# Rows 2 and 3 of a fused attention kernel: one tile of each pair transposed by VectorE and DMAs, diagonal blocks handled over their used columns, new timetables

## The reference

```
xn = layernorm(x)                                  # 8 x 1024 x 256
q = (xn @ Wq + bq) in 8 heads of 128, + positions  # one shared key/value head
k, v = xn @ Wkv + bkv, k + positions
scores = q k^T / sqrt(128), causal; probs = softmax(scores)
attn = (probs @ v) of 8 heads, side by side, @ Wo
r = sigmoid(xr @ W_r^T); kk = relu(xk @ W_k^T)^2   # xr, xk mix a token with the one before
out = x + attn + r * (kk @ W_v^T)
```

## Time and profile before

| | us |
|---|---|
| median of 3 runs (1560.83 to 1561.88) | 1561.39 |
| the profiled execution's own time | 1561.37 |
| its span in the profile | 1559.6 |
| PE busy | 1533.5 (98%) |
| PE weight loads busy (PEld) | 1497.6 (96%) |
| DVE busy | 1210.4 (78%) |
| ACT busy | 1056.2 (68%) |
| POOL busy | 1060.7 (68%) |

### The profile page before, as it was taken

How to read it: one execution, slowest core, us unless ns; L and a number is a source line. 1 busy time by engine, 2 the same in 40 slices (tenths; PEclk the granted TensorE clock), 3 DMA queues, 4 the chain that set the end, 5 groups by cost and what they waited for, 6 DMA issues and landing times.

```text
span 1559.6 us, 35317 instructions
## 1 busy us (share of the span) xinstructions
PE 1533.5 (98%) x12032; PEld 1497.6 (96%) x12032; DVE 1210.4 (78%) x3284; ACT 1056.2 (68%) x2531; POOL 1060.7 (68%) x1549
## 2 busy tenths in 40 slices
PE   5999999999999999999999999999999999999998
PEld 5999999999999999999999999999999999999998
DVE  6888767887678876788768787688876888768875
ACT  5776667766667766677577676676766677666764
POOL 5666776667756777567775676756766577765765
PEclk8999999999999999999999999999999999999999
DMA  4014420244202441024410244103431034300443
GB/s 139 9 53 121 146 75 22 58 122 148 69 15 69 129 143 55 15 75 134 144 42 15 86 141 127 42 15 98 140 129 32 12 112 138 129 20 8 119 147 105
DMA packets 151425, 132.46 MB, mean 85 GB/s; under 512 B 12240, under 2 KB 146512, under 8 KB 151248
## 3 DMA queue, kind: packets, MB, share of 16 engines
q1 hardware_dynamic: 150672, 129.55, 27.0%
q10 hardware_dynamic: 576, 0.66, 0.1%
HBM read 67.25 MB, written 62.91 MB: 83 GB/s over the span
## 4 chain that ended last, share of the span: by engine, by line
PE 76%; POOL 10%; issue 7%; DVE 5%; ACT 1%; DMA 0%; POOLq 0%; DVEq 0%; ACTq 0%
PE pS L893 25%; PE pO L893 23%; PE pG L893 19%; PE pT L986 8%; POOL qt L450 3%; POOL X L506 3%; DVE gate L698 1%; POOL pt L465 1%; POOL mh L456 1%; DVE X L872 1%; POOL rstd L434 1%; DVE mix L742 1%; POOL v L444 1%; POOL X L505 1%; DVE pt L797 1%
## 5 line engine op out<-in xcount | busy, mean ns | idle before, releaser
L893 PE MATMUL pO<-pt,v 128*128 128x256 f32 x3456 | 466.6, 285 | 6.5 <-DVE ot L848 5.3
L893 PE MATMUL pS<-kt,qt 128*128 128x288 f32 (+41 forms) x2304 | 458.6, 329 | 2.0 <-POOL qt L450 2.0
L659 ACT ACTIVATE X<-X,bias 128x16 f32<-128x16 f32 (+56 forms) x512 | 375.9, 734 | 93.3 <-DVE bias L872 92.8
L893 PEld LDWEIGHTS pO<-pt,v 128*128 128x128 f32 x3456 | 426.1, 189 | 12.1 <-DVE ot L848 10.0
L872 DVE CUSTOM_DVE_ANT_0 X<-pS,mask 128x16 f32<-128x16 f32 (+56 forms) x512 | 353.8, 691 | 45.1 <-issue 22.9
L506 POOL TENSOR_SCALAR X<-X,rec 128x16 f32<-128x16 f32 (+56 forms) x512 | 367.0, 717 | 23.0 <-DVE rec L780 23.0
L893 PEld LDWEIGHTS pS<-kt,qt 128*128 128x128 f32 x2304 | 367.5, 190 | 14.0 <-issue 2.2
L465 POOL TENSOR_TENSOR pt<-Z,pt 128x640 fp32r<-128x640 f32 (+3 forms) x128 | 256.6, 2005 | 63.3 <-ACT pt L588 61.6
L797 DVE TENSOR_TENSOR pt<-pT,pt 128x512 fp32r<-128x512 f32 (+3 forms) x512 | 257.3, 522 | 26.6 <-ACT pt L595 23.7
L595 ACT CAST pt<-pT 128x512 fp32r<-128x512 f32 (+3 forms) x512 | 223.0, 461 | 61.7 <-PE pT L986 58.8
L652 ACT CAST ot<-pO 128x256 fp32r<-128x256 f32 x256 | 96.2, 376 | 241.2 <-PE pO L893 115.0
(11 more groups left out here) (101 smaller groups left out, 1788.6 us busy)
## 6 DMA issues: line engine op xcount, KB each, us to landing
park_dram<-Y SPq DMA_DIRECT2D x32, 512.0 KB, 2.6
Z<-park_dram SPq DMA_DIRECT2D x128, 128.0 KB, 2.8
park_dram<-Y SPq DMA_DIRECT2D x32, 448.0 KB, 3.0
Z<-park_dram SPq DMA_DIRECT2D x128, 112.0 KB, 2.5
park_dram<-Y SPq DMA_DIRECT2D x32, 384.0 KB, 2.9
Z<-park_dram SPq DMA_DIRECT2D x128, 96.0 KB, 2.3
park_dram<-Y SPq DMA_DIRECT2D x32, 320.0 KB, 2.7
Z<-park_dram SPq DMA_DIRECT2D x128, 80.0 KB, 2.1
```

The source lines that it names most:

```text
L659: nc.scalar.activation(x_row(s, 0, w), x_row(s, 0, w), ACT.Exp, bias=bias[:, j:j + 1], scale=-1.0, accum_out=total[:, j:j + 1]).then_inc(e ...
L893: last = nc.tensor.matmul(out, a[i], m[j], start=start and k == 0, stop=stop and k == n - 1)
```

## The change

- `turned(s)` now holds for the even steps from 16 on, so 24 steps of a batch go by DVE and DMAs, not 16. The 8 new ones are in rows 2 and 3, with 3 and 4 blocks.
- The DMAs that read back write directly into `pt[1]`; ACT takes the high part from there, and POOL subtracts in place. `Z` is gone, `Y` has two buffers and the parked copy four. `pt` is laid out in pieces of 32 columns, and `pt[1]` has three pair slots. On SP the park is issued in turn s + 3 and the four reads in s + 4, both ahead of the stores of that turn.
- `diagonal(s)` is the used width of the diagonal block, rounded up to the pair: 32, 64, 96 or 128. TensorE transposes just these columns of the diagonal block, and the product with v takes just these rows of the last block (of v and of `pt`). POOL's memset shrinks to the 16 columns of an even step and goes for odd ones; in a DMA-transposed step it stays as it was. DVE clears both `pT` banks once at the start.
- `xnt` and `xt` have one buffer each, not two, with waits in `xt_out` for it.
- Timetables: `TURNS`, `WO_AT`, `AT`, `HALVES` have new numbers; `LEAD` is 10; WO stands ahead of the other products and of the product with v in its turn; DVE's and POOL's items are in another order within a turn. `scaled_by_act` is never true.

```diff
-LEAD = 12
+LEAD = 10
...
-WO_AT = (17, 25, 33, 41, 49, 57, 66, 72)
+WO_AT = (17, 26, 33, 41, 49, 56, 65, 73)
...
 def turned(s):
 
-    return s >= SHARED and s % 2 == 0
+    return s >= 16 and s % 2 == 0
...
+def diagonal(s):
+
+    return s % H // 2 * 2 * SUB + 2 * SUB
...
+            def fetch(b, s):
...
+                sp.wait_ge(parked[k % 2], 16 * (k // 2 + 1))
+                pair = b * (STEPS // 2) + s // 2
+                if pair >= PT_SLOTS[1]:
+                    sp.wait_ge(pv_done, pair - PT_SLOTS[1] + 1)
+                to = pt_of(1, b, s).bitcast(F)
                 for q in range(4):
+                    sp.dma_start(to[32 * q:32 * (q + 1), :, 0:nk, :].rearrange("r a k c -> r a (k c)"),
+                                 park_d[k % 4, :, q, 0:nk * 32].rearrange("(a r) n -> r a n", a=4)
+                                 ).then_inc(landed[k % 4], 16)
...
                         for i in range(nk):
-                            last = nc.tensor.transpose(pT[u % 2][:, i * P:(i + 1) * P],
-                                                       x_row(s, (k + i) * P, (k + i + 1) * P),
-                                                       ident[:, :])
+                            kn = P if k + i < s // H else diagonal(s)
+                            last = nc.tensor.transpose(pT[u % 2][0:kn, i * P:(i + 1) * P],
+                                                       x_row(s, (k + i) * P, (k + i) * P + kn), ident[:, :])
...
                     for k in ks:
-                        last = product(pO[:, 0:2 * P], [([x[:, k, :] for x in v], [x[:, pair % 2, k, :] for x in pt])],
+                        high, low = [x[:, (b * (STEPS // 2) + pair) % n, :, :, k, :].rearrange("p i a c -> p (i a) c")
+                                     for x, n in zip(pt, PT_SLOTS)]
+                        kn = P if k < nk - 1 else diagonal(2 * pair)
+                        last = product(pO[:, 0:2 * P], [([x[0:kn, k, :] for x in v], [high[0:kn], low[0:kn]])],
                                        start=k == 0, stop=k == nk - 1)
```

More of the change, by code:

```diff
@@ L102, in halves_of, with zeroed, turned_before, scaled_by_act @@
 def halves_of(s):
-    if s < SHARED:
-        return HALVES[s], 1
-    return (s // 2 % 2 * 2, 2) if turned(s) else ((s - SHARED) // 2 % 3 * 2 + 4, 2)
+    return HALVES[s], 1 if s < SHARED else 2
 def turned(s):
-    return s >= SHARED and s % 2 == 0
+    return s >= 16 and s % 2 == 0
+def diagonal(s):
+    return s % H // 2 * 2 * SUB + 2 * SUB
+def zeroed(s):
+    if turned(s):
+        return P - (s % H + 1) * SUB
+    return diagonal(s) - (s % H + 1) * SUB
+def turned_before(s):
+    j, n = halves_of(s)
+    found = []
+    for half in range(j, j + n):
+        back = 1
+        while not halves_of((s - back) % STEPS)[0] <= half < sum(halves_of((s - back) % STEPS)):
+            back += 1
+        if turned((s - back) % STEPS):
+            found.append((TURNED.index((s - back) % STEPS), s < back))
+    return found
+def scaled_by_act(s):
+    return s > 999
 def width(s):
@@ L138, in absent, with t_banks @@
     return c == NC and b == B - 1
+def t_banks(s):
+    n = s // H + 1
+    return [] if turned(s) else [(k, min(4, n - k)) for k in range(0, n, 4)]
 def users_before():
@@ L144, in users_before @@
     for b, it in turns():
+        if it >= T_LAG and it - T_LAG < STEPS:
+            order += [(b, ("T", it - T_LAG, m)) for m in range(len(t_banks(it - T_LAG)))]
         order += [(b, u) for u in FILL[it] if not absent(b, u[1])]
@@ L149, in users_before @@
     for b, u in order:
-        bank = u[1] % 2 + 1 if u[0] == "S" else G_BANK.get(u, 0)
+        if u[0] == "S":
+            bank = u[1] % 2 + 1
+        elif u[0] == "T":
+            bank = 3 + (T_FIRST[u[1]] + u[2]) % 2
+        else:
+            bank = G_BANK.get(u, 0)
         before[b, u] = last.get(bank)
@@ L470, in turn @@
                     if kind == "XT":
-                        split_xt(chunk_no(b, c), c % 2)
+                        split_xt(chunk_no(b, c))
+                for kind, c, p in FILL[it - 2] if it > 1 else []:
+                    if absent(b, c):
+                        continue
+                    if kind == "Q":
+                        split_q(chunk_no(b, c), c % 2, p, 1)
+                for kind, c, p in FILL[it - 1] if it else []:
+                    if absent(b, c):
+                        continue
+                    if kind == "Q":
+                        split_q(chunk_no(b, c), c % 2, p, 0)
+                    elif kind == "KV" and c < NC:
+                        split_v(chunk_no(b, c), c)
                 c, i = it // PER, it % PER
```

286 lines of the change are left out of this document (143 added, 143 removed).

## The result

| | before | after | ratio, 95% interval |
|---|---|---|---|
| median, us | 1561.55 | 1601.97 (1599.83 to 1604.78, 4 runs) | 1.026 (1.0247 to 1.0273) |
| profiled span, us | 1559.6 | 1598.1 | |
| matmuls on TensorE | 12,032 | 11,808 | |

The forecast was 1533 us, in a range of 1522 to 1566. The measured time lies above the range and the direction is wrong. Rival B, the cost of changes of array rows, is what happened, with two smaller costs beside it.

What follows compares the result with a forecast made beforehand. TensorE's gapless stream of matmuls was taken to bound the kernel, its time following from their number and pace. 1561.4 - 24.6 (transposes) - 8.0 (narrow ones) + 0 + 4.0 (waits) gave 1533 us, range 1522 to 1566.

Steps and rivals of the forecast that it cites:

- Rival B: Changes of array rows in products with v cost: 1554 us at half the drain, 1575 at all; 15% below break-even, 11% above.
- Transposes that go: On TensorE, 224 transposes of eight steps a batch leave at 110 ns each: 24.6 us saved.
- Narrow diagonal transposes: Diagonal blocks on TensorE load 32, 64 or 96 columns, so shorter loads save 8.0 us, ends 0 and 10.0.
- Products over fewer rows: The last block's products with v over 32 to 128 rows: no gain, row changes cost 0, upper end 42.5 us.
- Moving operand in pieces: Products with v read the moving operand as 8 pieces of 32 columns, not 256 in one: taken as 0.
- The other engines: Added work on DVE, ACT and POOL brings waits of 0.5 us a batch, 4 us; ends 0 and 24.
- The deadline of pair 8: The first pair using a newly DMA-transposed step, 16: ready at 644.7, needed at 645.5, a margin of 0.8 us.
- Sum: For the whole kernel, 1561.4 - 24.6 - 8.0 + 0 + 4.0 = 1532.8, given as 1533 us, 1.8% faster.
- rival A: The forecast's own range for the whole kernel, 1522 to 1542 us: narrow transposes, waits and `ot` vary; 53%.

Runs made afterwards that it cites:

- e8_before_turned16: The kernel before, with only the even steps 16 to 30 also turned by VectorE and DMAs, in its old tables and layout: 1592.99 us, ratio 1.0203.
- e13_both: The changed kernel with full 128-wide diagonal blocks, transposed weights in 256-column pieces, and steps 26 and 30 left to TensorE: 1550.58 us, ratio 0.9925.
- e5_narrow_only: The changed kernel with its narrow transposes kept but the products with v over all 128 rows: 1562.2 us, ratio 0.9999.
- e3_full128: The changed kernel with all 128 rows and columns used on the diagonal: 1565.65 us, ratio 1.0021.
- e2b: The kernel before, with only the third of the last block's three matmuls over its used rows: 1599.17 us, ratio 1.024.
- e2: The kernel before, with all three matmuls of the last block of each product with v over its used rows: 1600.91 us, ratio 1.025.
- e1_rows96: The changed kernel with at least 96 rows and columns used on the diagonal, never 32 or 64: 1566.75 us, ratio 1.003.
- e7: The changed kernel with full 128-wide diagonal blocks and the output projection behind the product with v of its turn: 1568.91 us, ratio 1.005.

## Why the prediction was wrong, step by step

- **Transposes that go**, - 24.6 us: the count is right (x1248). Alone, in the old tables and buffers, it gave + 31.5 us (`e8_before_turned16`), of which near 12 are the lower granted clock behind the longer waits, and in `e13_both`, with 160 transposes fewer (17.6 us at 110 ns), - 10.7 with waits left. No run shows the number by itself.
- **Narrow diagonal transposes**, - 8.0 (0 to 10.0): measured - 2.6 in `e5_narrow_only`, inside the range by luck, since the reason given does not hold. A narrow transpose starts 109 ns behind its neighbour as a full one does, so in these kernels what paces transposes does not go with their columns; that the load is the limit was inferred by exclusion. The prediction also cited the Trainium skill (TensorE: Matmul & The Clock Gate, section on LDWEIGHTS) for that. By its rule, as an estimate, 32 columns load in a quarter of the time of 128; the recorded loads take 97 ns against 140, so they shrink much less, and the pace of 109 ns does not shrink at all. The measurement decides.
- **Products over fewer rows**, taken as 0, upper end 42.5: this is the step that failed. It measured 39.6 us in the kernel's time, 155 ns a change. Where it stands a change costs 193 ns, more than the 166 that was held to be the most; less idle time elsewhere hid the difference. The reason for taking 0 was that changes from transpose to product cost nothing. Those all use 128 rows: they say nothing on a change of rows. The only evidence in favour of 0 was about another kind of change, and the range ended at 1566 although a bound worked out by the text itself reached 1575. The rule of the Trainium skill (TensorEngine Tiling, Key Properties), that a change of tiling mode drains TensorE, agrees with the loss at 32 and 64 rows; 96 rows behave as 128.
- **Moving operand in pieces**, taken as 0: measured + 8.9, 2.6 ns a matmul. That no matmul of the trace reads so was true, and 3456 instructions multiply any small price.
- **The other engines**, + 4 (0 to 24): mis-sized, measured 15.1 for the two steps that were taken back, and in the wrong place. The deadline of pair 8, whose margin was worked out at 0.8 us, held: no wait for `pt` stands among TensorE's ten longest. The late engine was VectorE at turns 32 to 34, where the last DMA-turned steps of row 3 meet the chunk's normalisation. The sums of busy time were right in kind. In the changed kernel's window that answers to the earlier trace rows,

```profile
642.80:680.70 37.90, 37.90 (x286) 36.03 (x286) 30.30 (x99) 27.08 (x74) 26.75 (x43) 1.00 0.26 74
```

  VectorE is busy for 30.30 us of 37.90, 80% where 88% was forecast, and GpSimd for 26.75, 71% where 80% was. Work lags its step by up to 7 turns, so the subtractions of steps 26 to 30 and the transpose of step 30 fell outside the window that was looked at, into the next chunk, and a share of busy time does not show that one engine's operation holds up another's.
- **Sum.** 1561.4 - 24.6 - 2.6 + 39.6 + 8.9 + 15.1 = 1597.8, against 1602.0 measured. The 4.2 us left are not attributed; no run takes the new timetables, the single buffers of `xnt` and `xt` or the clearing of `pT` by themselves, which were all taken as 0. The terms are not quite independent, since TensorE's lateness hides waits: the wait for `xtok` is 12.1 us in `e3_full128` and 8.9 in the changed kernel.

One slip in the working changed nothing: the upper end of rival A is 1561.4 - 24.6 + 4 + 5 = 1546 by its own terms, not 1542.

What the prediction named as its signs fitted. 100 ns or more beyond 118 between a 32-row matmul and its neighbours was to show B; in the changed kernel 212 ns pass to the first start of a run of small products and 226 to the second (medians of 128 runs), 94 and 108 beyond it. Busy time did not fall by 30 us but rose, and the starts in the stream of `pO` lay 121 ns apart, over the 120 that it named; those belong to the pieces.

## What to carry to other kernels

If no row shows a thing, bounds from other rows are all there is: do not choose the end that the mechanism you hope for needs, above all when the count is in the hundreds. Multiplying over fewer partitions saved nothing here, since the streamed columns set the time, and it cost at each switch. So keep the full 128, with zeros in the unused rows (96 did as well). To group the small ones would make fewer changes; no run here tried it. When work leaves the bounding engine, follow each operation of its substitute to the turn in which it runs, not to the step it belongs to, and look there for what it stands beside and what stands behind it. Read the granted clock of every run before its waits are taken for the whole of its loss.

## What the runs showed of the hardware

- A change between 128 rows and 64 or 32 delays TensorE by 190 to 200 ns where it stands, in two parts: + 92 ns ahead of the next matmul, + 105 ahead of the one after. In the time of these kernels it came to 145 to 174 ns, since other idle time shrank. It was the same with one and with three small matmuls between two changes (e2b and e2).
- 96 rows cost next to nothing: around a run of three products over 96 rows the starts of `e1_rows96` are 7 ns later in all than those of `e3_full128` (median of 192 runs), against 384 ns for 32 or 64.
- Transposes that load 32, 64 or 96 columns start 109 ns behind the one before, as full ones, though their loads are recorded as 97, 111 and 125 ns against 140.
- A moving operand of 256 columns in 8 pieces of 32 costs 2 to 3 ns a matmul more than in one.
- A VectorE operation on two inputs in SBUF that started beside GpSimd's subtraction lasted until 0.29 us after its end: 1506 ns instead of 473, and 2068 ns beside a longer subtraction in the kernel before.
- TensorE's granted clock fell to 0.50, for 3.4 us or more, during or just behind 7 of 8 waits of 2.85 us (e8) and 3 of 8 waits of 2.0 us (e7); each fall of 3.4 us cost near 1.5 us.
